# Two adjacency pairs kept on chip over the turn of a two-pass graph kernel, and one pair moved from the fourth step to the first

## The chip, the cores and the metric

The kernel runs on one core of one Trainium2 chip. The metric is the device time of one execution in microseconds, the median over several runs; lower is better.

## What is computed

The graph has 4096 nodes of 64 features and a dense 4096 x 4096 f32 adjacency matrix (64 MB). The reference, cut to what matters:

```python
def _ggc(x, adj, W, wih, whh, bih, bhh):
    m = adj @ (x @ W)
    gi = m @ wih.T + bih ; gh = x @ whh.T + bhh      # each split in three: r, z, n
    r = sigmoid(i_r + h_r); z = sigmoid(i_z + h_z); n = tanh(i_n + r * h_n)
    return (1.0 - z) * n + z * x

# layer 0: two passes over adj, with a residual and a layernorm
h = relu(_ggc(x, adj, W1, ...)) ; x = layernorm(x + relu(_ggc(h, adj, W2, ...)))
# layer 1: decayed weights of the last 100 neighbours of each row
support = x @ weight ; mask = adj != 0 ; rank = cumsum(mask, axis=1)
k = minimum(rank[:, -1:], 100) ; pos = rank - (deg - k)
w = mask * where(pos > 0, 0.5 ** (k - pos), 0)
x = layernorm(x + w @ support + bias)
```

## The kernel before, in words

The adjacency doesn't fit on the chip, so it is streamed. It is cut in 8 chunks of 512 output nodes, each chunk in 16 **pairs**; a pair is 256 source nodes by 512 output nodes, 512 KB of f32, and it is what one DMA loads and what one product of TensorE takes (four matmul records and four weight loads, helper `pair`, L445 to L451). `LOADS` (L74) lists all loads in order and `LOAD_AT` gives the place n of a pair in it. Load n goes to slot n % 7 of `stream`, a ring of seven slots. SyncE issues all of them (`load`, L390): load n waits until the pair n - 7 has been multiplied (`pair_used`), and in pass 1 until its mask has been made as well. The loads are in one queue and SyncE issues them strictly in this order.

**Pass 1** (loads 0 to 127) goes through chunks 0 to 7. For each pair VectorE (or, for some, ScalarE by a Sign and a Square) makes the 8-bit mask `codes`, and TensorE multiplies the pair with the first state `s_in`. The second state `s_mid` of a chunk is ready one chunk later, so pairs with source nodes below `2 * TRI[b]` are at once multiplied with it too, which saves a second load (L457 to L466). In chunk 7, pairs 0 to 11 are used twice in this way; pairs 12 to 15 of chunk 7 are not.

**The turn** (`TURN`, L72, and L607 to L614) is the first part of pass 2: twelve pairs in an order written out by hand. The tuple (s, q) is step s of pass 2, that is chunk 7 - s, pair q. It begins with (0, 12) and (0, 13), two pairs of chunk 7, which are loaded again as loads 128 and 129. Between its products lie `gates(7)`, `count(7)` and `node(7)`, the end of pass 1's last chunk.

**Pass 2** goes backwards through the chunks, with the loads 140 to 203, in six steps `chunk2(t)` (L616 to L627). Step t first runs `gates(7 + t)`, then `ALONG_PAIRS[t]` products, with `node(7 + t)` after the fourth of them. From step 2 on, four shares of layer 1's product (`share`, L540; each 16 matmuls of 128x128 f16) go with them, two ahead of the first product and two ahead of the fifth. Before: `{1: 8, 2: 10, 3: 12, 4: 12, 5: 11, 6: 11}`. A product needs its load, and steps run over chunk borders freely; so the counts say only how many pairs lie between two gates. After step 6 come 44 more shares, with the last two gates and nodes among them (L631 to L636).

What joins the engines around one chunk g of pass 2:

- TensorE's `gates(g)` (L497, matmuls of L509 and L516) waits for `m_ready` (VectorE, `combine`, L979), `state_made` (ScalarE, L701), `h_made` (VectorE, L1010) and, for g of 9 and up, `x1_made` (VectorE, `make_x1s`, L1073).
- ScalarE then makes the sigmoids `rz` (L678), VectorE `t_n` (L988, L992), ScalarE tanh (L685), VectorE `new_h` (L999 to L1004) and `residual` (L1010), which writes `h_c`.
- TensorE's `node(g)` (L522, L531) needs `h_c`; ScalarE squares it (L721), VectorE sums it (L1062, L1066), GpSimd takes the power (L851), VectorE makes `x1s` (L1073), ScalarE and VectorE split it (L731, L1089).
- Between these VectorE works off a written-out list of `chain` steps (L955, L960: the running count over the rows, and the codes) and ScalarE and VectorE expand codes to weights for the shares (L741 and L1100). Each engine takes its list strictly in order; VectorE's per-step list is at L1121 to L1142, ScalarE's at L799 to L811.

`RES_AT` (L105) sets after which load SyncE issues the small load `x_res` that `residual` needs.

On-chip memory that the change touches: `wexp` holds two buffers for expanded weights; its first half serves as `sums` in pass 1, its second half is used from step 1 of pass 2 on. `h_c` (L236), `sq` (L237) and `x1s` (L238) are 1, 1 and 2 KB per partition, 4 KB in all, the size of a pair per partition, and are written from step 1 of pass 2 on.

Of the kernel before, what the change touches and what calls it, by code (L numbers as in the profile page):

```python
# [17 lines left out]
P = 128  # L18
# [52 lines left out]

TURN = [(0, 12), (0, 13), (1, 10), (1, 11), (1, 12), (1, 13), (2, 10), (0, 14), (0, 15),  # L72
        (1, 14), (1, 15), (2, 11)]
LOADS = [(b, q) for b in range(NCH) for q in PAIRS[b]] + [(NCH + s, q) for s, q in TURN] + \  # L74
        [(NCH + s, q) for s in range(2, NCH) for q in range(2 * TRI[NCH - 1 - s], NP)
     if (s, q) not in TURN]
LOAD_AT = {pair: n for n, pair in enumerate(LOADS)}
# [21 lines left out]

ALONG_PAIRS = {1: 8, 2: 10, 3: 12, 4: 12, 5: 11, 6: 11}
FIRST = [NCH * NP, *(NCH * NP + len(TURN) + sum(ALONG_PAIRS[u] for u in range(1, t))
                     for t in range(1, NCH))]
RES_AT = [FIRST[1], *(n + SLOTS + 3 for n in FIRST[1:NCH - 1]), len(LOADS)]  # L105

# [64 lines left out]
OUT_ACT = (0, 2, 4)  # L171


def signed(n):
    return n % NP in BY_SIGN.get(n // NP, ())

# [28 lines left out]
def build(nc, adj_t, x_pairs, w1, consts, bias, out):  # L205
    with ExitStack() as ctx:
# [3 lines left out]
        def sem(name):  # L210
            return ctx.enter_context(nc.semaphore(name))
# [21 lines left out]
        zh = r_g  # L233
        n_g = sb("n_g", [P, HW], F32)
        x_res = sb("x_res", [P, HW], F32)
        h_c = sb("h_c", [P, HW], F32)  # L236
        sq = sb("sq", [P, KT, D], F32)  # L237
        x1s = sb("x1s", [P, KT, 2, D], F32)  # L238
        x1, sup_f = x1s[:, :, 0, :], x1s[:, :, 1, :]
        stat = sb("stat", [P, NCH, KT], F32)  # L240
        var = sb("var", [P, NCH, KT], F32)
# [82 lines left out]
        def support(j):  # L324
# [6 lines left out]
                at = s_mid[:, 0:CW].bitcast(F16)[:, (j - 6) * CW:(j - 5) * CW]  # L331
            return at.rearrange("p (k h d) -> p k h d", h=2, d=D)

        def edges(c, b, first, n):

            at = (c * NCH + b) * BLK + first * CW
            return codes[:, at:at + n * CW]
# [21 lines left out]
        x_in = [sem(f"x_in{i}") for i in range(len(X_IN))]  # L359
        w1_in, consts_loaded, bias_in = sem("w1_in"), sem("consts_loaded"), sem("bias_in")  # L360
        adj_in = [sem(f"adj_in{i}") for i in range(SLOTS)]
        pair_used, mask_made, sum_made = sem("pair_used"), sem("mask_made"), sem("sum_made")
        signs_read, squares_made = sem("signs_read"), sem("squares_made")
        s_bf_made, count_done, start_made = sem("s_bf_made"), sem("count_done"), sem("start_made")
# [23 lines left out]
        @blk.sync  # L388
        def _(sp):
            def load(n):  # L390
                g, q = LOADS[n]
                if n >= SLOTS:
                    sp.wait_ge(pair_used, n - SLOTS + 1)
                    if n - SLOTS < NCH * NP:
                        by_dve, by_sign = masks_before(n - SLOTS + 1)
                        if signed(n - SLOTS):
                            sp.wait_ge(signs_read, by_sign)
                        else:
                            sp.wait_ge(mask_made, by_dve)
                sp.dma_start(stream[:, n % SLOTS, :], adj_t[g if g < NCH else 2 * NCH - 1 - g, q])\  # L400
                    .then_inc(adj_in[n % SLOTS], 16)

            def load_res(s):
                ch, g = NCH - 1 - s, NCH + s
                if s > 0:
                    sp.wait_ge(h_made, g)
                sp.dma_start(x_res[:, :], x_pairs[:, bass.ts(ch, HW)]).then_inc(x_c_in, 16)

            for b in range(NCH):
                for q in range(NP):  # L410
                    load(b * NP + q)
                    if b == BIAS_AT - 1 and q == NP - 1:
                        sp.dma_start(bias_b[:, :, :].rearrange("p k d -> p (k d)"), bias)\
                            .then_inc(bias_in, 16)
            for n in range(NCH * NP, len(LOADS)):
                load(n)
                for s in range(NCH):
                    if n == RES_AT[s]:
                        load_res(s)
            load_res(NCH - 1)  # L420
            for i in range(NCH):
                if i in OUT_ACT:
                    sp.wait_ge(o_by_act, OUT_ACT.index(i) + 1)
                else:
                    sp.wait_ge(o_by_dve, i + 1 - sum(a < i for a in OUT_ACT))
                sp.dma_start(out[NCH - 1 - i], o_n[:, i]).then_inc(out_stored, 16)
            sp.wait_ge(out_stored, 16 * NCH)

        @blk.tensor
        def _(pe):  # L430
# [12 lines left out]
                last.then_inc(xw_done, 1)  # L443

            def pair(n, q, state, to, start, stop):  # L445
                for u in range(2):
                    t = 2 * q + u
                    last = nc.tensor.matmul(to[D * u:D * (u + 1), :], state[:, t * D:(t + 1) * D],  # L448
                                            stream[:, n % SLOTS, u * CW:(u + 1) * CW],
                                            start=start[u], stop=stop)  # L450
                return last  # L451

            def product1(b, q):
                n = LOAD_AT[b, q]
                pe.wait_ge(adj_in[n % SLOTS], 16 * (n // SLOTS + 1))
                last = pair(n, q, s_in, m_acc[b % 2], [q == PAIRS[b][0]] * 2, q == PAIRS[b][-1])
                twice = [p for p in PAIRS[b] if p < 2 * TRI[b]]  # L457
                if q in twice:
                    first = q == twice[0]
                    pe.wait_ge(s_mid_made, q // 2 + 1)  # L460
                    if first:
                        if b == 5:
                            pe.wait_ge(to_sup_made, 4)
                        if b in M2_AFTER:
                            pe.wait_ge(m2_kept, KEPT.index(M2_AFTER[b]) + 1)
                    last = pair(n, q, s_mid, m2_bank(b), [first] * 2, q == twice[-1] and b in KEPT)  # L466
                last.then_inc(pair_used, 1)

            def product2(s, q):
                g, ch = NCH + s, NCH - 1 - s  # L470
                n = LOAD_AT[g, q]
                first = s >= 3 and q == 2 * TRI[ch]
                pe.wait_ge(s_mid_made, q // 2 + 1)
                if first:

                    pe.wait_ge(m_ready, {3: NCH, 4: NCH - 1}.get(s, s + 7))
                pe.wait_ge(adj_in[n % SLOTS], 16 * (n // SLOTS + 1))
                pair(n, q, s_mid, acc_bank(g), [first] * 2, n == USED[g] - 1).then_inc(pair_used, 1)
                if first and ch in KEPT:
                    half, _, at = kept_part(ch)  # L480
# [158 lines left out]
        def _(act):  # L639
# [16 lines left out]
            def sign_mask(b, q):  # L656
                n, p = b * NP + q, PAIRS[b][q]
                to = edges(p // 2, b, 2 * (p % 2), 2)
                act.wait_ge(adj_in[n % SLOTS], 16 * (n // SLOTS + 1))
                nc.scalar.activation(to.bitcast(I8), stream[:, n % SLOTS, :], ACT.Sign)\  # L660
                    .then_inc(signs_read, 1)
                act.wait_ge(signs_read, masks_before(n)[1] + 1)
                nc.scalar.activation(to, to.bitcast(I8), ACT.Square).then_inc(squares_made, 1)
# [195 lines left out]
        def _(dve):  # L859
# [47 lines left out]

            def mask(b, q):
                n, p = b * NP + q, PAIRS[b][q]
                dve.wait_ge(adj_in[n % SLOTS], 16 * (n // SLOTS + 1))  # L910
                nc.vector.tensor_scalar(edges(p // 2, b, 2 * (p % 2), 2), stream[:, n % SLOTS, :],  # L911
                                        0.0, None, ALU.not_equal).then_inc(mask_made, 1)

            def sum_quads(b, part):
# [305 lines left out]
```

## Time and profile before

| | us |
|---|---|
| median of 3 runs | 353.23 |
| lowest and highest run | 352.85, 354.26 |
| the profiled execution, its own time | 352.96 |
| its span, first to last instruction | 351.2 |
| granted TensorE clock over the span | 0.998 of 2.4 GHz |

The time of the profiled execution is 1.8 us over its span; these lie outside the program's instructions. How to read the rows: busy times and starts are in microseconds from the start of the span, mean durations in ns. PE is the matmul side of TensorE, PEld its weight loads, DVE VectorE, ACT ScalarE, POOL GpSimd, SP SyncE. L448 is line 448 of the kernel. In a timeline a row is a run of instructions of one kind; the brackets at its end give the idle time of the engine ahead of it and what ended it, and a row without brackets followed the one before it with no idle time to speak of. Matmuls are pipelined, their ends are modelled and a pair's records overlap the next pair's, so the spacing of starts tells the rate, not the duration.

### The profile page before, as it was taken

What the parts mean: (1) busy time and instruction counts of PE and PEld (TensorE: products, weight loads), DVE (VectorE), ACT (ScalarE), POOL (GpSimd) and SP (SyncE); (2) the same over time, 40 slices, a digit from 0 to 9 for tenths busy, and PEclk for the clock granted to TensorE, in tenths of its full rate; (3) what the DMA queues carried; (4) which work ended last, traced back from release to release, by engine and by line L of the source; (5) the groups of instructions that cost most, each with busy time, mean ns of one, the idle gap of its engine ahead of it and who ended that gap; (6) DMA issues with size and microseconds to landing.
All of it is one profiled execution on the core that took longest, in us unless ns stands there. A gap on an engine that the chain in (4) does not pass through costs nothing. (4 is left out here: it accounts for less than half of the span.)

```text
span 351.2 us, 6769 instructions
## 1 busy us (share of the span) xinstructions
PE 329.9 (94%) x2536; PEld 154.2 (44%) x2536; DVE 302.4 (86%) x510; ACT 180.7 (51%) x235; POOL 24.8 (7%) x32
## 2 busy tenths in 40 slices
PE   1997999999999999999999999999999999979992
PEld 0441323233333333333333324444444454869992
DVE  0689879898999999997995667899899999888996
ACT  0202403114031140367467448977996969676993
POOL 2000000000000000000000001202020202022044
PEclk9999999999999999999999999999999999999999
DMA  7999999999999999999899999999999995000012
GB/s 243 413 411 410 410 407 409 409 409 397 405 361 331 392 377 363 365 318 342 294 359 316 376 411 406 406 350 326 358 380 370 383 383 215 17 1 4 2 32 91
DMA packets 32720, 111.10 MB, mean 316 GB/s; under 512 B 3632, under 2 KB 6192, under 8 KB 32688
## 3 DMA queue, kind: packets, MB, share of 16 engines
q1 hardware_dynamic: 31824, 109.20, 82.2%
q10 hardware_dynamic: 864, 1.48, 1.2%
q8 instruction: 20, 0.33, 0.4%
q14 instruction: 12, 0.10, 0.1%
HBM read 109.62 MB, written 1.05 MB: 315 GB/s over the span
## 5 line engine op out<-in xcount | busy, mean ns | idle before, releaser
L448 PE MATMUL m_acc<-stream,s_in 128*64 128x512 f32 x512 | 126.7, 603 | 4.0 <-DMA stream<-in_adj_t 3.1
L911 DVE TENSOR_SCALAR codes<-stream 128x1024 uint8<-128x1024 f32 x117 | 77.1, 686 | 6.6 <-DMA stream<-in_adj_t 6.3
L448 PE MATMUL out<-stream,s_mid 128*64 128x512 f32 x272 | 68.5, 593 | 0.2 <-DMA stream<-in_adj_t 0.2
L448 PEld LDWEIGHTS m_acc<-stream,s_in 128*64 128x64 f32 x512 | 34.4, 138 | 70.9 <-issue 47.9
L448 PE MATMUL m_acc<-stream,s_mid 128*64 128x512 f32 x240 | 55.2, 599 | 0.1
L851 POOL TENSOR_TENSOR rstd<-var,mhalf 128x4 f32<-128x4 f32 x16 | 23.0, 1436 | 322.7 <-DVE var L1066 322.7
L960 DVE SCALAR_TENSOR_TENSOR codes<-codes,run 128x384 uint32<-128x384 uint32 (+2 forms) x56 | 43.0, 768 | 1.9
L955 DVE TENSOR_TENSOR run<-run,codes 128x768 uint16<-128x768 uint16 (+2 forms) x55 | 41.5, 755 | 1.8
L646 ACT ACTIVATE m_high<-m_acc 64x512 f32<-64x512 f32 x13 | 7.7, 596 | 58.0 <-PE m_acc L448 45.1
L448 PEld LDWEIGHTS out<-stream,s_mid 128*64 128x64 f32 x272 | 19.5, 137 | 38.1 <-issue 37.4
L678 ACT ACTIVATE rz<-gate_ps,b_rz 128x256 f32<-128x256 f32 x32 | 13.4, 469 | 43.7 <-PE gate_ps L516 43.6
L741 ACT ACTIVATE wexp<-codes,code_bias 128x2048 uint16<-128x2048 uint8 x15 | 29.8, 1996 | 0.1
L741 ACT ACTIVATE codes<-codes,code_bias 128x2048 uint16<-128x2048 uint8 x15 | 29.6, 1989 | 0.0
L448 PEld LDWEIGHTS m_acc<-stream,s_mid 128*64 128x64 f32 x240 | 15.8, 136 | 28.9 <-issue 27.7
L928 DVE TENSOR_TENSOR wexp<-wexp,codes 128x2048 uint16<-128x2048 uint16 x16 | 19.6, 1225 | 6.5 <-issue 6.0
L509 PE MATMUL gate_ps<-mx,const 128*64 128x256 f32 x128 | 16.8, 381 | 2.1 <-DVE x1s L1073 2.0
L509 PEld LDWEIGHTS gate_ps<-mx,const 128*64 128x64 f32 x128 | 9.5, 137 | 13.2 <-issue 9.3
L685 ACT ACTIVATE n_g<-t_n,const 128x256 f32<-128x256 f32 x16 | 8.2, 511 | 13.3 <-DVE t_n L992 12.9
L1100 DVE TENSOR_SCALAR codes<-codes 128x2048 uint16<-128x2048 uint8 x12 | 14.3, 1221 | 0.0
L701 ACT ACTIVATE mx<-hx 64x256 f32<-64x256 f32 x32 | 13.3, 416 | 0.8
L863 DVE COPY s_in<-gate_ps 128x256 f32<-128x256 f32 x8 | 3.4, 420 | 11.3 <-PE gate_ps L440 11.3
L988 DVE SCALAR_TENSOR_TENSOR t_n<-gate_ps,const,rz 128x256 f32<-128x256 f32 x16 | 7.7, 481 | 6.1 <-ACT rz L678 5.9
(139 smaller groups left out, 375.2 us busy)
## 6 DMA issues: line engine op xcount, KB each, us to landing
stream<-in_adj_t SPq DMA_DIRECT2D x204, 512.0 KB, 6.4
x_res<-in_x_pairs SPq DMA_DIRECT2D x8, 128.0 KB, 6.8
out_nodes<-stream SPq DMA_DIRECT2D x8, 128.0 KB, 2.1
hx<-in_x_pairs ACTq DMA_DIRECT2D x1, 512.0 KB, 7.5
const<-in_consts ACTq DMA_DIRECT2D x1, 358.0 KB, 6.7
hx<-in_x_pairs ACTq DMA_DIRECT2D x2, 128.0 KB, 6.1
hx<-in_x_pairs ACTq DMA_DIRECT2D x1, 256.0 KB, 8.8
bias_b<-in_bias SPq DMA_DIRECT2D x1, 128.0 KB, 5.4
```

What stands on the lines that cost most here:

```text
L448: last = nc.tensor.matmul(to[D * u:D * (u + 1), :], state[:, t * D:(t + 1) * D], stream[:, n % SLOTS, u * CW:(u + 1) * CW], start=start[u] ...
L509: nc.tensor.matmul(to[e * D:(e + 1) * D, 0:HW], w_rz[layer][:, part * D:(part + 1) * D], mx[:, e * HW:(e + 1) * HW], start=True, stop=True)
L678: nc.scalar.activation(rz[:, bass.ts(part, HW)], (r_ps, z_ps)[part], ACT.Sigmoid, bias=b_rz[:, 2 * layer + part:2 * layer + part + 1])\
L685: nc.scalar.activation(n_g[:, :], t_n[:, :], ACT.Tanh, bias=b_ni[:, layer:layer + 1]).then_inc(n_made, 1)
L701: nc.scalar.activation(mx[D:P, e * HW:(e + 1) * HW], state_of(g)[e * D:(e + 1) * D, :], ACT.Copy)\
L741: nc.scalar.activation(weights(j, i).bitcast(U16), block(j, i), ACT.Relu, bias=code_bias[:, :], scale=float(P)).then_inc(by_act, 1)
L851: nc.gpsimd.tensor_tensor(rstd[:, r, :], var[:, r, :], mhalf[:, :], ALU.pow) .then_inc(rstd_made, 1)
L911: nc.vector.tensor_scalar(edges(p // 2, b, 2 * (p % 2), 2), stream[:, n % SLOTS, :], 0.0, None, ALU.not_equal).then_inc(mask_made, 1)
L928: nc.vector.tensor_tensor(to, left, right, ALU.add).then_inc(sum_made, 1)
L955: nc.vector.tensor_tensor(running(n + 1, U16)[:, to], running(n, U16)[:, to], tile_edges(c, k, U16)[:, to], ALU.subtract)\
L960: nc.vector.scalar_tensor_tensor(at, at, EDGE_BIT, running(n, U32)[:, to], ALU.logical_shift_left, ALU.bitwise_or)\
L1100: nc.vector.tensor_scalar(weights(j, i).bitcast(U16), block(j, i), float(P), -float(P * CODE_ZERO), ALU.mult, ALU.add)\
```

## The change

Pairs 12 and 13 of chunk 7 are loaded in pass 1 not into the ring but each into a place of its own: pair 12 into the second half of `wexp`, pair 13 into a new tile `late` of 4 KB per partition, of which `h_c`, `sq` and `x1s` become parts. The two loads of pass 2 for them go, 202 loads are left. The held loads have semaphores of their own, SyncE issues them without waiting for a slot, and their products in the turn neither wait for a load nor count as used. `landing(n)` counts what has been loaded into a slot, since the held loads leave theirs out. Products, masks and their order in pass 1 and in the turn are the same. `ALONG_PAIRS` goes to nine pairs in step 1 and eleven in step 4; steps 2 and 3 keep their counts, so that each of their pairs is the next one in the order.

```diff
+HELD = (12, 13)
+HELD_AT = [(NCH - 1) * NP + PAIRS[NCH - 1].index(q) for q in HELD]
+TURN_LOADS = [(NCH + s, q) for s, q in TURN if (s, q) not in [(0, p) for p in HELD]]
-LOADS = [(b, q) for b in range(NCH) for q in PAIRS[b]] + [(NCH + s, q) for s, q in TURN] + \
+LOADS = [(b, q) for b in range(NCH) for q in PAIRS[b]] + TURN_LOADS + \
...
-ALONG_PAIRS = {1: 8, 2: 10, 3: 12, 4: 12, 5: 11, 6: 11}
-FIRST = [NCH * NP, *(NCH * NP + len(TURN) + sum(ALONG_PAIRS[u] for u in range(1, t))
+ALONG_PAIRS = {1: 9, 2: 10, 3: 12, 4: 11, 5: 11, 6: 11}
+FIRST = [NCH * NP, *(NCH * NP + len(TURN_LOADS) + sum(ALONG_PAIRS[u] for u in range(1, t))
...
+def landing(n):
+
+    return 16 * sum(m not in HELD_AT for m in range(n % SLOTS, n + 1, SLOTS))
...
-        h_c = sb("h_c", [P, HW], F32)
-        sq = sb("sq", [P, KT, D], F32)
-        x1s = sb("x1s", [P, KT, 2, D], F32)
+        late = sb("late", [P, PW], F32)
+        h_c = late[:, 0:HW]
+        sq = late[:, HW:2 * HW].rearrange("p (k d) -> p k d", d=D)
+        x1s = late[:, 2 * HW:4 * HW].rearrange("p (k h d) -> p k h d", h=2, d=D)
+        held = [wexp[:, 1, :].bitcast(F32), late[:, :]]
...
+        def loaded(n):
+
+            if n in HELD_AT:
+                return held[HELD_AT.index(n)]
+            return stream[:, n % SLOTS, :]
+
+        def pair_in(engine, n):
+            if n in HELD_AT:
+                engine.wait_ge(held_in[HELD_AT.index(n)], 16)
+            else:
+                engine.wait_ge(adj_in[n % SLOTS], landing(n))
...
+        held_in = [sem(f"held_in{i}") for i in range(len(HELD))]
...
             def load(n):
                 g, q = LOADS[n]
+                if n in HELD_AT:
+                    at = HELD_AT.index(n)
+                    sp.dma_start(held[at], adj_t[g, q]).then_inc(held_in[at], 16)
+                    return
                 if n >= SLOTS:
...
             def pair(n, q, state, to, start, stop):
+                data = loaded(n)
...
-                                            stream[:, n % SLOTS, u * CW:(u + 1) * CW],
+                                            data[:, u * CW:(u + 1) * CW],
...
             def product2(s, q):
                 g, ch = NCH + s, NCH - 1 - s
+                if s == 0 and q in HELD:
+                    pe.wait_ge(s_mid_made, q // 2 + 1)
+                    pair(LOAD_AT[ch, q], q, s_mid, acc_bank(g), [False] * 2, False)
+                    return
                 n = LOAD_AT[g, q]
...
-                pe.wait_ge(adj_in[n % SLOTS], 16 * (n // SLOTS + 1))
+                pair_in(pe, n)
```

The waits and operands of the products of pass 1 and of the masks (L455, L659, L910) go through `pair_in` and `loaded` in the same way.

## Rows read from the trace of the kernel before

**Rows 1.** The page: engines' busy time in us, share of the span, instructions.

```profile
PE 329.9 (94%) x2536; PEld 154.2 (44%) x2536; DVE 302.4 (86%) x510; ACT 180.7 (51%) x235; POOL 24.8 (7%) x32
```

**Rows 2.** Windows: length, busy (x records) of PE, PEld, DVE, ACT, POOL; clock; DMA share; GB/s.

```profile
192.00:216.00 24.00, 23.48 (x136) 7.52 (x132) 16.89 (x39) 12.44 (x20) 1.14 (x1) 1.00 1.01 393
...
206.00:216.20 10.20, 9.83 (x58) 2.94 (x55) 7.74 (x19) 7.20 (x10) 1.14 (x1) 1.00 1.03 410
```

**Rows 3.** Waits of PE from 190 to 300 us: total, times, longest (all there are).

```profile
PE gate_ps L509 <- DVE x1s L1073: 0.4, 1, 0.4
PE out L448 <- DMA stream<-in_adj_t: 0.2, 1, 0.2
```

**Rows 4.** Chain of waits: start, length, what; products between two gates.

```profile
242.96 5.30 PE m_acc L448 x24
...
260.46 6.16 PE m_acc L448 x28
```

**Rows 5.** Timeline of PE, end of the turn and step 1 of pass 2.

```profile
204.12 1.08 PE L448 MATMUL out<-stream,s_mid 128*64 128x512 f32 x4 [0.21 <-DMA stream<-in_adj_t]
205.31 1.08 PE L509 MATMUL gate_ps<-mx,const 128*64 128x256 f32 x8
...
210.62 0.72 PE L531 MATMUL gate_ps<-to_x1s,h_c 64*128 64x128 f32 x8
...
212.85 2.96 PE L448 MATMUL m_acc<-stream,s_mid 128*64 128x512 f32 x12
216.17 1.08 PE L509 MATMUL gate_ps<-mx,const 128*64 128x256 f32 x8 [0.37 <-DVE x1s L1073]
```

**Rows 6.** Timeline of DVE, the same stretch: `combine(8)` and `make_x1s(0)`.

```profile
204.59 0.67 DVE L979 TENSOR_TENSOR mx<-out,m_high 64x512 f32<-64x512 f32 x1
...
215.34 0.68 DVE L1073 TENSOR_TENSOR x1s<-gate_ps,rstd 128x512 f32<-128x512 f32 x1
```

**Rows 7.** Pair loads: 22 issued 190 to 220 us; one at 208.9; one at 179.6.

```profile
DMA to landing us min/median/max: 5.1/6.9/9.1
...
DMA to landing us min/median/max: 7.0/7.0/7.0
...
DMA to landing us min/median/max: 4.4/4.4/4.4
```

**Rows 8.** Timeline of DVE, steps 2 to 7: the rows with a wait, and `n_input(14)`.

```profile
218.77 0.48 DVE L988 SCALAR_TENSOR_TENSOR t_n<-gate_ps,const,rz 128x256 f32<-128x256 f32 x1 [1.04 <-ACT rz L678]
...
224.44 0.42 DVE L1062 TENSOR_REDUCE stat<-sq 128x4 f32<-128x256 f32 x1 [0.44 <-ACT sq L721]
...
252.16 0.48 DVE L988 SCALAR_TENSOR_TENSOR t_n<-gate_ps,const,rz 128x256 f32<-128x256 f32 x1 [0.64 <-ACT rz L678]
...
267.34 1.22 DVE L1100 TENSOR_SCALAR codes<-codes 128x2048 uint16<-128x2048 uint8 x1
268.66 0.48 DVE L988 SCALAR_TENSOR_TENSOR t_n<-gate_ps,const,rz 128x256 f32<-128x256 f32 x1
...
274.67 0.42 DVE L1062 TENSOR_REDUCE stat<-sq 128x4 f32<-128x256 f32 x1 [0.16 <-ACT sq L721]
...
301.55 0.48 DVE L988 SCALAR_TENSOR_TENSOR t_n<-gate_ps,const,rz 128x256 f32<-128x256 f32 x1
```

**Rows 9.** Timeline of ACT: `sigmoids(11)`, one expansion, `sigmoids(14)`.

```profile
251.67 0.81 ACT L678 ACTIVATE rz<-gate_ps,b_rz 128x256 f32<-128x256 f32 x2
...
288.24 2.01 ACT L741 ACTIVATE wexp<-codes,code_bias 128x2048 uint16<-128x2048 uint8 x1
...
299.41 0.84 ACT L678 ACTIVATE rz<-gate_ps,b_rz 128x256 f32<-128x256 f32 x2 [0.56 <-PE gate_ps L516]
```

**Rows 10.** Timeline of PE: end of `gates(11)`; after the last product, `gates(15)` and `node(15)`.

```profile
250.20 0.66 PE L516 MATMUL gate_ps<-mx,const 64*64 64x256 f32 x8
...
310.49 1.08 PE L509 MATMUL gate_ps<-mx,const 128*64 128x256 f32 x8 [1.64 <-DVE x1s L1073]
...
316.35 0.71 PE L531 MATMUL gate_ps<-to_x1s,h_c 64*128 64x128 f32 x8 [0.51 <-DVE h_c L1010]
```

More of the change, by code:

```diff
@@ L476, in product2 @@
                     pe.wait_ge(m_ready, {3: NCH, 4: NCH - 1}.get(s, s + 7))
-                pe.wait_ge(adj_in[n % SLOTS], 16 * (n // SLOTS + 1))
+                pair_in(pe, n)
                 pair(n, q, s_mid, acc_bank(g), [first] * 2, n == USED[g] - 1).then_inc(pair_used, 1)
@@ L658, in sign_mask @@
                 to = edges(p // 2, b, 2 * (p % 2), 2)
-                act.wait_ge(adj_in[n % SLOTS], 16 * (n // SLOTS + 1))
-                nc.scalar.activation(to.bitcast(I8), stream[:, n % SLOTS, :], ACT.Sign)\
+                pair_in(act, n)
+                nc.scalar.activation(to.bitcast(I8), loaded(n), ACT.Sign)\
                     .then_inc(signs_read, 1)
@@ L909, in mask @@
                 n, p = b * NP + q, PAIRS[b][q]
-                dve.wait_ge(adj_in[n % SLOTS], 16 * (n // SLOTS + 1))
-                nc.vector.tensor_scalar(edges(p // 2, b, 2 * (p % 2), 2), stream[:, n % SLOTS, :],
+                pair_in(dve, n)
+                nc.vector.tensor_scalar(edges(p // 2, b, 2 * (p % 2), 2), loaded(n),
                                         0.0, None, ALU.not_equal).then_inc(mask_made, 1)
```

## The prediction

> **What bounds the kernel now.** I began with the page: PE is busy for 94% of the span, DVE for 86% [rows 1], so one of these two sets the time nearly everywhere, and DMA matters only where it makes one of them wait. The windows come next: through the turn and step 1 (192 to 216 us) the DMA engines are fully busy at 393 to 410 GB/s [rows 2], so here the removed loads could count. Then I asked what PE waited for in pass 2. There is little: 0.2 us for a pair's load and 0.4 us for DVE's `x1s`, each once, in 110 us [rows 3]. Last I followed DVE: from 224.44 to 301.55 its row of work has two waits in it, 0.64 us at 252.16 and 0.16 us at 274.67 [rows 8]. So PE and DVE run beside each other, both nearly full, and a gain on one counts only as far as the other lets it through. That is the main point of what follows.
>
> **Who sets the end.** PE starts `node(15)` at 316.35 after waiting for DVE's `h_c`, and `gates(15)` at 310.49 after waiting 1.64 us for DVE's `x1s` [rows 10]. Both hang on the chain that starts with `n_input(14)` on DVE at 301.55. That one did not wait: it has no bracket, and its sigmoid had started at 299.41, 2.1 us before [rows 8, 9]. DVE itself was late there. So the last 50 us move with DVE's start of `n_input(14)`, not with the end of PE's last product.
>
> **Part 1, the held pairs in pass 1.** Masks and products are the same in number and shape, from another address; 0. The two held loads are issued earlier than before (no slot wait) in a stretch where a load lands 4.4 us after its issue (the third of [rows 7]) and PE never waits; 0. If a held load did delay a neighbour by its own length, 1.3 us, PE's lead there would have to be gone first.
>
> **Part 2, two loads less in the turn.** A pair is 524288 bytes; at 410 GB/s [rows 2] that is 1.28 us, so the queue carries 2 x 1.28 = 2.56 us less. What reaches the loads behind is less. Loads for the next seven pairs go into slots freed in pass 1, and come two places, 2.56 us, earlier. But the pair after those, (1, 14), goes into the slot that (1, 10) frees, and that product is where it was. Before, it also had that slot. It is issued at the same time as before, and so is all behind it. It can only lose its queueing: it landed 5.1 us after its issue (the smallest of the 22 in [rows 7]), and an unqueued load takes 4.4 us. So from there on loads land 0.7 us earlier, not 2.56. Between 0 (if the queue is no shorter) and 0.7 I take 0.7, by the nearer row, as the queue is empty for a moment there.
>
> What does that bring PE? The product at 204.12 waited 0.21 us for its load [rows 5]. That wait goes. But `gates(8)` at 205.31 stands right behind `combine(8)` on DVE, 204.59 + 0.67 = 205.26 [rows 5, 6], and that stands behind DVE's chain steps, which no load touches. So the 0.21 us are given back in front of `gates(8)`: 0. `node(8)` at 210.62 and `x1s` at 215.34 hang on `gates(8)` alone: unmoved.
>
> The Trainium skill speaks of a shorter load than the row: "SBUF — State Buffer", section The DMA setup-cost knee, gives a transfer as about 2 us plus its bytes at 436 GB/s, 3.2 us for this size. By that, an estimate, loads behind the turn would land 1.9 us earlier and not 0.7; the trace has 4.4 us for one that waits for nothing, so it does not agree. The sum would be the same by either, only the slower rival below would lose most of its chance.
>
> **Part 3, the ninth pair in step 1.** A product costs PE (6.16 - 5.30) = 0.86 us [rows 4]. After `node(8)` the last three products start at 212.85 and 0.86 us apart; PE is through at 212.85 + 3 x 0.86 = 215.43, with small overheads 215.6, and waits until 216.17 for `gates(9)`, where DVE's `x1s` ends at 215.34 + 0.68 = 216.02 [rows 5, 6]. So PE has a hole of 0.55 to 0.6 us (the row shows 0.37, as a matmul record ends later than the next could start). A product of 0.86 us put into it ends at 212.85 + 4 x 0.86 = 216.29, with the overhead of about 0.05 216.34. `gates(9)` thus starts 0.17 us later: +0.17. Its load is the one issued at 208.9, landing at 215.9 before (the second of [rows 7]), at 215.2 after; it is needed at 215.5. It fits by 0.3 us.
>
> DVE's `n_input(9)` at 218.77 had waited 1.04 us for the sigmoids [rows 8], so it takes over the 0.17, and so does the sum of squares at 224.44 (it waited 0.44 for `node(9)`). From there DVE runs without a wait to 251.5: it is +0.17 all along. The wait at 252.16 gives nothing back: the sigmoid before it, at 251.67, has no bracket, so ScalarE came straight from an expansion [rows 9], and that row of expansions began with DVE's `x1s`. Steps 2 and 3 in all: +0.17.
>
> **Part 4, one pair less in step 4.** PE's `gates(12)` comes 0.86 us earlier, less the 0.17: -0.7. What does DVE take of that? At 268.66 `n_input(12)` follows an expansion from 267.34 of 1.22 us, which overlaps with the next by 0.08 elsewhere, so it could have started at 268.47: 0.19 us. At 274.67 it waited for the square behind `node(12)`, 0.16 us by the row, 0.25 with the same overlap [rows 8]. Behind that there is no wait on DVE up to 301.55 [rows 8]. So DVE can take at most 0.19 + 0.25 = 0.44 us of PE's 0.7, and keeps it to the end. The rest becomes idle time of PE: shares of step 6 use an expansion that ends only at 288.24 + 2.01 = 290.25 [rows 9], and ScalarE starts it by DVE's pace, and after 300 us PE waits for `h_c` and `x1s` longer.
>
> Moved with the pairs: `x_res` loads follow the same pairs or one later, and two or more steps of DVE lie before their use; 0. One pair is multiplied earlier in steps 1 to 3, so its successor's load has a slot 0.86 us earlier as well. Should a load in step 3 stall PE all the same, by up to 0.8 us it would only shrink PE's -0.7 and not reach DVE: `gates(11)` ends at 250.20 + 0.66 = 250.86 [rows 10], and ScalarE comes to its sigmoid at 251.67 [rows 9]. ScalarE's `high` and DVE's `combine` find their chunks done one pair earlier or at the same time, and the power on GpSimd waits for DVE alone: 0.
>
> **Sum.** DVE: +0.17 - 0.44 = -0.27 us, against 352.96 us of the profiled execution: 352.7. The median of the runs before is 0.27 us above that execution, so the median expected is 353.23 - 0.27, about 352.9. What a measurement of this kernel can tell from no change is about 0.5%, 1.8 us, so this is no change.
>
> **The rivals.**
>
> *PE sets the end after all* (0.15). If DVE's list is looser than its rows look (its durations overlap by up to 0.08 us, in some 60 instructions), then PE's 0.7 us comes through: 352.5. For it: PE is unbroken from 216 to 300 us. Against it: the 2.1 us by which the sigmoid of step 7 lay ready.
>
> *DMA sets the pace* (0.05). The loads run through pass 2 at the rate of full engines; if they did bound it, the whole 2.56 us would come off: 350.7. "Perfetto Trace Analysis" of the Trainium skill, section Roofline, puts the ceiling of one core at about 435 GB/s, and by that rule the 393 to 410 GB/s of the turn are near the bound. Against it stands the 0.2 us that PE waited for loads in pass 2 [rows 3]; the trace disagrees with this rule's outcome.
>
> *The ninth pair comes too late, and the kernel gets slower* (0.2). Place: the last product of step 1. If the loads are not earlier at all (the queue as before), its load lands at 215.9, PE takes it some 0.1 us later, and `gates(9)` starts at 216.9: +0.7 us, and everything up to the end hangs on `gates(9)` through DVE. With the 0.44 taken back in step 4 that is +0.3, 353.5. Loads of this stretch took up to 9.1 us [rows 7], 2.1 more than this one; with half of that on it the sum is +1.3, 354.5. It decides from a landing after 215.5 on, 0.3 us later than I expect it. For it: a margin of 0.3 us only. Against it: the queue must be shorter by two loads somewhere.
>
> **How the numbers follow.** The forecast (-0.27) has 0.6; its own range is 352.5 to 353.3. Rivals 0.15, 0.05 and 0.2. The range reaches from 352.1 (rival 1 with the spread of the medians, 0.4 us) to 353.9 (rival 3 with its smaller price and the same spread). Faster by over 0.5%: 0.05 from DMA and 0.02 for what I have not seen; slower by over 0.5% only in rival 3 beyond its larger price: 0.03. The rest, 0.90, is within 0.5%.
>
> **What would show it.** Right: no PE wait for a load in the turn; `gates(8)` at the same time; `gates(9)` 0.1 to 0.3 us later, with no wait before it; the last product 0.4 to 0.7 us earlier, but `n_input(14)` only 0.2 to 0.3 us earlier; more PE idle time before `node(14)` and `gates(15)`. Wrong: a wait for a load at the ninth pair; `gates(8)` earlier; `n_input(14)` earlier by 0.6 or more; any DVE wait in steps 5 to 7.

## The result and the profile after

The changed kernel takes 354.73 us (median of 8 runs, 354.56 to 355.27) against 353.34 us before (8 runs): a ratio of 1.0038, with a 95% interval of 1.0025 to 1.0051. It is 1.4 us slower, inside the half per cent that counts as no change, but outside the predicted range, and with the other sign. The profiled execution has 354.69 us of its own, its span is 353.0 (before 352.96 and 351.2). The ratios here and below leave out three executions that lie far off the rest (495 us in e1, 879 us in e9, 1931 us of the kernel before beside e13 and e14).

The page of the changed kernel, engines' busy time, shows that the work is the same as in [rows 1]:

```profile
PE 329.6 (93%) x2536; PEld 154.2 (44%) x2536; DVE 302.4 (86%) x510; ACT 180.5 (51%) x235; POOL 24.8 (7%) x32
```

What it waits for is not. PE's waits from 190 to 300 us in the changed kernel, to be held against [rows 3]:

```profile
PE m_acc L476 <- DMA stream<-in_adj_t: 1.7, 2, 0.9
PE gate_ps L541 <- DVE mx L1011: 0.6, 1, 0.6
PE out L595 <- ACT wexp L773: 0.2, 1, 0.2
PE m_acc L476 <- issue: 0.2, 1, 0.2
```

Two loads less, and PE now waits 1.7 us for loads where it had waited 0.2. The larger of the two waits, 0.92 us, is that of the ninth pair of step 1; the other, 0.76 us at the end of step 3, did no harm, since DVE's `n_input(11)` behind it waits 0.63 us as before (0.64). (Line numbers have moved: 476 is the product, 541 and 548 the gates, 516 the kept sums' product, 563 the node, 1020 `n_input`, 1094 the sum of squares.) The timeline of PE at the end of the turn and in steps 1 and 2 answers to [rows 5]:

```profile
205.05 1.08 PE L541 MATMUL gate_ps<-mx,const 128*64 128x256 f32 x8 [0.55 <-DVE mx L1011]
...
212.57 2.96 PE L476 MATMUL m_acc<-stream,s_mid 128*64 128x512 f32 x12
216.44 1.08 PE L476 MATMUL m_acc<-stream,s_mid 128*64 128x512 f32 x4 [0.92 <-DMA stream<-in_adj_t]
217.32 1.06 PE L541 MATMUL gate_ps<-mx,const 128*64 128x256 f32 x8
...
220.80 3.65 PE L476 MATMUL m_acc<-stream,s_mid 128*64 128x512 f32 x16
224.38 0.65 PE L516 MATMUL m_acc<-kept,ident 64*64 64x256 f32 x4
224.96 0.72 PE L563 MATMUL gate_ps<-to_x1s,late 64*128 64x128 f32 x8
```

Everything up to `gates(8)` is 0.26 us earlier than before, `gates(7)` too (193.33 against 193.59). Executions differ by that much before they reach the turn, so I count from `gates(7)` below. Two things are to be seen. The ninth product of step 1 starts at 216.44, 0.92 us after PE had nothing else to do. And in step 2 the product of the kept sums (L516) stands ahead of `node(9)` (L563): four products, then L516, then the node. Before, it stood behind it (L484 is the product, L531 the node):

```profile
223.26 0.72 PE L531 MATMUL gate_ps<-to_x1s,h_c 64*128 64x128 f32 x8
...
225.79 1.08 PE L448 MATMUL m_acc<-stream,s_mid 128*64 128x512 f32 x4
226.80 0.65 PE L484 MATMUL m_acc<-kept,ident 64*64 64x256 f32 x4
```

The timeline of DVE, the rows with a wait and two `n_input` rows, to be held against [rows 8]:

```profile
219.55 0.48 DVE L1020 SCALAR_TENSOR_TENSOR t_n<-gate_ps,const,rz 128x256 f32<-128x256 f32 x1 [2.09 <-ACT rz L710]
226.14 0.42 DVE L1094 TENSOR_REDUCE stat<-late 128x4 f32<-128x256 f32 x1 [1.36 <-ACT late L753]
...
253.78 0.48 DVE L1020 SCALAR_TENSOR_TENSOR t_n<-gate_ps,const,rz 128x256 f32<-128x256 f32 x1 [0.63 <-ACT rz L710]
260.10 0.42 DVE L1094 TENSOR_REDUCE stat<-late 128x4 f32<-128x256 f32 x1 [0.48 <-ACT late L753]
...
270.67 0.48 DVE L1020 SCALAR_TENSOR_TENSOR t_n<-gate_ps,const,rz 128x256 f32<-128x256 f32 x1
...
303.28 0.48 DVE L1020 SCALAR_TENSOR_TENSOR t_n<-gate_ps,const,rz 128x256 f32<-128x256 f32 x1
```

The sum of squares of step 2 waits 1.36 us for its node (before 0.44), and there is a wait of 0.48 us at the same place of step 4 (260.10) that did not exist. `n_input(14)` is at 303.28 and not at 301.55, +1.73; the span is 1.7 longer. The end still hangs on it: in all profiles of this study but one it lies 49.68 to 49.70 us behind `n_input(14)`, and 49.73 in that one.

**Where the saved transfers went.** Windows of the kernel before and of the changed kernel over the turn; the columns are those of [rows 2]. Before:

```profile
195.00:197.00 2.00, 2.00 (x15) 0.75 (x12) 0.90 (x2) 1.34 (x3) 0.00 (x0) 1.00 0.99 401
197.00:201.00 4.00, 4.00 (x26) 1.49 (x24) 2.60 (x7) 2.72 (x6) 0.00 (x0) 1.00 1.00 404
201.00:206.00 5.00, 4.67 (x24) 1.37 (x22) 3.81 (x9) 0.60 (x1) 0.00 (x0) 1.00 1.02 408
```

After:

```profile
195.00:197.00 2.00, 2.00 (x12) 0.76 (x14) 1.09 (x3) 1.33 (x4) 0.00 (x0) 1.00 0.47 188
197.00:201.00 4.00, 4.00 (x28) 1.48 (x26) 2.66 (x7) 2.46 (x6) 0.00 (x0) 1.00 0.94 303
201.00:206.00 5.00, 4.45 (x26) 1.31 (x22) 3.57 (x8) 0.59 (x1) 0.00 (x0) 1.00 0.99 362
```

The difference is 2 x 213 + 4 x 101 + 5 x 46 = 1060 KB, two pairs. The transfers that were taken away became an idle queue at 195 us, and then a queue that restarts slowly; by 206 us the kernel has moved two pairs less than before, just those that were taken away, and the loads land when they did.

### The profile page after: what moved, and what is told of

The parts are those of the page before. It is cut to its first block and busy times, and to the rows that moved or that the text cites. A ratio compares the mean times of both kernels' runs of the same rounds, so it can differ in the third digit from the quotient of the medians.

```text
span 353.0 us, 6763 instructions
## 1 busy us (share of the span) xinstructions
PE 329.6 (93%) x2536; PEld 154.2 (44%) x2536; DVE 302.4 (86%) x510; ACT 180.5 (51%) x235; POOL 24.8 (7%) x32
## 5 line engine op out<-in xcount | busy, mean ns | idle before, releaser
L476 PE MATMUL m_acc<-stream,s_in 128*64 128x512 f32 x504 | 124.8, 604 | 3.9 <-DMA stream<-in_adj_t 3.1
L476 PE MATMUL out<-stream,s_mid 128*64 128x512 f32 x264 | 66.5, 593 | 0.0
```

## The experiments

For each run the table gives, for its profiled execution: its own time; the landing of the ninth pair of step 1, chunk 4's pair 12, and the start of `gates(9)`, both counted from `gates(7)`; from there to step 2's sum of squares; and from that to `n_input(12)`. Then the ratio to the kernel before over all runs, with its interval.

| | own | landing | gates(9) | to squares | to n_input(12) | ratio |
|---|---|---|---|---|---|---|
| before | 352.96 | 22.29 | 22.58 | 8.26 | 44.22 | |
| change | 354.69 | 22.98 | 24.00 | 8.82 | 44.52 | 1.0038 (1.0025 to 1.0051) |
| e1 hold only | 352.78 | 22.74 | 22.59 | 8.26 | 44.04 | 0.9992 (0.9978 to 1.0006) |
| e2 move only | 353.95 | 22.32 | 23.33 | 8.82 | 44.53 | 1.0064 (1.0040 to 1.0087) |
| e3 kept sums behind node | 354.91 | 23.34 | 24.35 | 9.11 | 43.96 | 1.0015 (1.0001 to 1.0030) |
| e4 held pairs later | 354.79 | 22.73 | 23.74 | 8.82 | 44.53 | 1.0028 (1.0013 to 1.0043) |
| e5 more waits | 355.64 | 23.11 | 24.12 | 8.82 | 44.52 | 1.0062 (1.0038 to 1.0085) |
| e6 change, node after 3 | 353.31 | 22.56 | 23.57 | 7.68 | 44.60 | 1.0020 (1.0002 to 1.0037) |
| e7 before, node after 3 | 353.19 | 22.50 | 22.58 | 8.04 | 44.77 | 1.0012 (0.9997 to 1.0028) |
| e8 e4 and e6 | 352.90 | 21.66 | 22.67 | 7.94 | 44.34 | 0.9996 (0.9985 to 1.0007) |
| e9 e8, pair from step 2 | 352.44 | 21.06 | 22.62 | 7.99 | 43.96 | 0.9983 (0.9966 to 1.0000) |
| e10 change, again | 355.86 | 24.24 | 25.25 | 8.82 | 44.52 | one run |
| e11 move only, again | 354.59 | 22.60 | 23.62 | 8.88 | 44.52 | one run |
| e12 as e5, other semaphore | 355.35 | 23.04 | 24.05 | 8.82 | 44.52 | 1.0068 (1.0048 to 1.0089) |
| e13 ninth without load | 353.69 | 22.84 | 22.63 | 8.79 | 44.53 | 1.0028 (1.0016 to 1.0041) |
| e14 e13, kept sums behind | 353.59 | 23.41 | 24.01 | 8.24 | 43.95 | 1.0007 (0.9996 to 1.0017) |

The columns nearly tell it by themselves: where the ninth pair is in step 1, and loaded, `gates(9)` comes 1.01 or 1.02 us after its landing in all but one (in e9 the load is in time); 8.8 stands where the kept sums' product is ahead of `node(9)`, about 8.25 where it is behind and nothing else waits.

**e1: hold, move nothing.** The counts are those of before.

```diff
-ALONG_PAIRS = {1: 9, 2: 10, 3: 12, 4: 11, 5: 11, 6: 11}
+ALONG_PAIRS = {1: 8, 2: 10, 3: 12, 4: 12, 5: 11, 6: 11}
```

> The two pairs are held, the counts of the steps stay 8, 10, 12, 12. Theory A (the loss sits in the moved pair: its load comes late, and the product with the kept sums, 0.58 us, slips ahead of node(9)): no change against before, within 0.3 us; gates(8), gates(9) and n_input(14) where they were, relative to gates(7), and the product at the end of the turn without its wait of 0.2 us. Theory B (holding itself costs, by the addresses or by the queue that runs empty at 196 us): slower than before by about the 1.4 us of the change.

0.9992, no change: theory B falls. Holding costs nothing and brings nothing. Its product at the end of the turn still waited 0.2 us for a load, so theory A was not right in that either.

**e2: move, hold nothing.** The reverse edit in the kernel before.

> Nothing is held, the kernel before with nine pairs in step 1 and eleven in step 4. Theory A: as slow as the change, 1.0 to 2.0 us over before; the ninth pair waits for its load, 0.5 to 1.3 us, and node(9) comes 1.1 to 1.8 us later. Theory C (holding did bring the loads 0.7 us forward, and the rest of the loss is elsewhere): 0.7 us slower than the change, 2.1 us over before.

1.0064: the moved pair alone is the loss. The size, 2.3 us by the medians (355.28 against 352.98), was theory C's and above A's; C's reason isn't borne out, since the ninth pair's load landed no later here (22.32) than with holding (22.98). Its profiled execution was the fastest of its six; the second look, e11, came out nearer the others. Whether holding makes the moved pair cheaper (1.0038 against 1.0064, with intervals that overlap) these runs don't settle: the landing is 22.3 and 22.6 us without holding, 22.98 and 24.24 with it.

**e3: the kept sums' product behind the node.** The four matmuls that add the kept sums are no longer issued with the chunk's first product but ahead of the next one, so behind a node that falls between:

```diff
                 if first and ch in KEPT:
-                    half, _, at = kept_part(ch)
-                    pe.wait_ge(m2_kept, len(KEPT))
...
+                    kept_due.append((g, ch))
...
                     if n == NODE_AT[t]:
                         node(NCH + t - 1)
+                    add_kept()
```

> The change, with the product of the kept sums put behind node(9), node(10) and node(11) in place of ahead of them. Theory A: node(9) and the sum of squares behind it come 0.55 us earlier than in the change, and since VectorE waited there, so does the end: 0.5 us faster than the change. Theory D (only the late load counts): as slow as the change within 0.2 us.

1.0015 against 1.0038, 0.8 us by the ratios, with intervals that overlap a little: it speaks against theory D, the product counts. This profile is that of its slowest run, with another late load of 0.65 us ahead of `node(9)`, so its 9.11 hides the gain; the next column shows it, 43.96 against 44.52. The same product slips ahead of `node(11)` in step 4 as well. e14 shows both.

**e4: held pairs later in the turn.**

```diff
-TURN = [(0, 12), (0, 13), (1, 10), (1, 11), (1, 12), (1, 13), (2, 10), (0, 14), (0, 15),
+TURN = [(1, 10), (1, 11), (1, 12), (0, 12), (0, 13), (1, 13), (2, 10), (0, 14), (0, 15),
```

> The change, with the turn's two held pairs multiplied fourth and fifth in place of first and second, so that (1, 10), (1, 11) and (1, 12) free their slots about 3 us earlier. Theory A (the queue ran empty at 196 us because the held products free no slot, so the 2.56 us saved were lost as an idle queue): the queue stays full, loads of step 1 land 2 to 2.6 us earlier than in the change, the ninth pair does not wait, gates(9) is 1.2 us earlier, and the end 1.0 to 1.3 us earlier than in the change. Theory E (loads of that stretch are late for another reason, such as the engines being full): landings and time as in the change.

A part of it came. The load of (1, 15) landed 6.0 us after `gates(7)` and not 8.1, and that of (2, 11) at 7.3 and not 9.95, so the queue did stay full up to there, and theory E falls for this stretch. But (2, 12) was issued at 5.47 us as in the change and landed 3.5 us behind (2, 11): the queue had only run thin a place later. The lead was 0.85 us at (2, 12) and 0.56 at the eighth pair of step 1, since each load still has to wait for the product seven loads before it, and those products wait for gates and nodes, not for data. The ninth pair landed only 0.25 us earlier, 22.73, and the ratio is 1.0028, 0.35 us better and not 1.0 to 1.3.

**e5 and e12: where the instruction refill falls.** The profile of the changed kernel has one packet on the instruction queue in 213.9 to 214.5 us (columns: packets, MB, share of the 16 engines' time):

```profile
q1 hardware_dynamic: 66, 0.23, 96.0%
q8 instruction: 1, 0.02, 11.3%
```

There are 20 of these in the whole execution, 16 KB each and 0.9 to 1.1 us long on one DMA engine. The ninth pair's load was under way then, and it landed 2.0 us after its predecessor, where 1.28 is the rule. Two more waits per pair of pass 1 were to shift them:

```diff
+                    if b >= 1:
+                        pe.wait_ge(w1_in, 16)
+                        pe.wait_ge(w1_in, 16)
                     product1(b, PAIRS[b][q])
```

> The change, with two more waits ahead of each pair's products in chunks 1 to 7 of pass 1, on a semaphore that is long set. They hold nothing up; they only shift by some 224 instructions where TensorE's instruction stream is refilled (a 16 KB transfer on the instruction queue, at 214.1 us in the trace of the change). Theory F (such a refill, 1.1 us on one DMA engine, made the ninth pair's load late): the refill comes at about 217 us, that load lands 1.0 us after its predecessor's 1.3 us and not 2.0, the product waits under 0.4 us, and the time is 0.5 to 1.0 us below the change. Theory E (late for another reason): wait and time of the ninth pair as in the change, 0.9 us by the row and 354.7.

A miss. The refill came at 205.0 us, and the time got worse, 1.0062. There were 21 refills and not 20, which ties this queue to TensorE's instructions, the only ones that the edit adds. But the program as built has 2116 instructions for TensorE against 2004 of the change: one more for each pair and not two, as the other wait is carried by an instruction that was there already. A second kernel had the second wait on another semaphore, which was to give two each:

> The change with two waits on two different semaphores ahead of each pair of chunks 1 to 7 (in e5 the two were on one semaphore and became one, 112 instructions in all). Theory F: with 224 instructions the refills fall 32 instructions, some 3 us, later than in the change, at about 217.5 us and behind the ninth pair's load, whose product waits at most 0.3 us; time 353.6 to 354.2. Rival: where the refill falls isn't set by the instruction count, and it comes in front of the load as in the change: 354.7 or more.

Another miss, and the run isn't what was expected of it: this program too has 2116 instructions for TensorE, 112 more than the change and not 224. It repeats e5. The refill fell 13.7 us after `gates(7)`, at 207.6, ahead of the load once more; 1.0068. So a program with 224 more was never run, and I couldn't place a refill where I wanted it.

What the profiles say together is more. Counted from the landing of (2, 13), seven loads ahead, the ninth pair's load lands 8.9 to 9.0 us later in twelve of the sixteen profiles, that is at the pace of seven times 1.28. In the other four it takes 9.7 (change), 9.9 (e13), 10.05 (e4) and 10.5 us (e10), and these are the four in which a refill falls 19.4 to 20.8 us after `gates(7)`, while this load or the one ahead of it was under way. In the others the refill falls elsewhere and the gap with it: in twelve profiles, these four among them, a pair lands 1.9 to 3.2 us behind its predecessor, 2.2 to 3.3 us after a refill began. In the other four the refill of e14 has no such gap behind it, that of e3 begins when its gap is nearly over, and those of e5 and e12 fall ahead of (2, 13), which there lands 2.5 us behind (2, 12). So a refill goes with 0.7 to 1.5 us on the ninth pair's landing; it is not shown to be the cause, as no run moved it at will.

The rest of the spread lies in (2, 13) itself, which lands at 13.3 to 13.7 us without holding and at 12.2 to 14.5 with it. In e1, e3, e10 and e14 it came 2.7 to 3.0 us behind (2, 12), before 1.64, with no refill near. That is why e3 and e14 landed late (23.3 and 23.4) with no refill in the stretch.

**e10: the change again.**

> The changed kernel itself, a second execution under the profiler. If the refill of TensorE's instructions falls before the ninth pair's load again (214.1 us in the first profile, 219.7 in e6 with the same program up to there), that load is late again, 0.9 us of wait, and the time is about 354.7; if it falls after it, the wait is 0.2 us and the time 353.6 to 354.0.

A refill in the stretch again (19.9 us after `gates(7)`), and the load later still. PE of that profile waits twice:

```profile
216.33 1.08 PE L476 MATMUL m_acc<-stream,s_mid 128*64 128x512 f32 x4 [1.49 <-DMA stream<-in_adj_t]
217.62 1.08 PE L476 MATMUL m_acc<-stream,s_mid 128*64 128x512 f32 x4 [0.20 <-DMA stream<-in_adj_t]
```

**e11: move only, again.**

> e2's kernel again (nothing held, pair moved), since its profiled execution was its fastest (353.95 against a median of 355.28). Expected now: the ninth pair's load lands 1 us or more later than the 22.3 us after gates(7) of that profile, by a refill or a queue that was late before it, and the product waits 1 us or more.

Landing 22.60, 0.3 us later than in e2's profile and not 1 us; `gates(9)` 23.62, time 354.59. A miss in size, but with e2 it shows the floor: even a load that no refill makes late holds `gates(9)` up by 0.75 us (e2) to 1.04 us (e11) against 22.58.

**e6: node one product earlier, in the change.**

```diff
-NODE_AT = {1: 4, 2: 4, 3: 4, 4: 4, 5: 4, 6: 4}
+NODE_AT = {1: 4, 2: 3, 3: 3, 4: 3, 5: 4, 6: 4}
```

> The change, with node(9), node(10) and node(11) after three products of their step in place of four, so ahead of the chunk's first product and of the kept sums' product. Theory A: node(9) comes 0.86 + 0.58 us earlier, VectorE's sum of squares takes the 1.36 us it had waited for it, and the end is 1.0 to 1.4 us earlier than in the change, close to before. Theory D (only the late load counts): as slow as the change within 0.3 us.

The squares come 7.68 us behind `gates(9)` and not 8.82, as said, and the time falls to 1.0020, 0.65 us by the ratios where I had 1.0 to 1.4: A was too large. Over its own runs of the kernel before, the median is 1.08 us slower, where the change had 1.39; by that measure the gain is 0.3 us, on the edge of what D allows. The rows, not the time of this run, speak against D.

**e7: the same in the kernel before.**

> The kernel before with the same three nodes one product earlier. Theory A (VectorE sets the end from step 2 on, its wait of 0.44 us at the sum of squares of step 2 is the only one left): 0.4 to 0.5 us faster than before. Rival (TensorE sets the end): no change.

No gain: 1.0012, the outcome of the rival. The squares are earlier (8.04), but then DVE's `n_input(10)` waits where it had not waited:

```profile
233.99 0.48 DVE L988 SCALAR_TENSOR_TENSOR t_n<-gate_ps,const,rz 128x256 f32<-128x256 f32 x1 [0.35 <-ACT rz L678]
```

Its sigmoid follows `gates(10)` on PE. In step 2 both engines are at the end of their slack, and what is taken from one the other asks for: the 0.2 us that DVE gained at the squares is gone at `n_input(10)`, so DVE doesn't set the pace alone.

**e8: both.**

> The change with the held pairs fourth and fifth in the turn and the three nodes one product earlier. Theory A: both gains of e4 and e6 in one, 353.0 to 353.6, no slower than before. Rival: the gains overlap, since both shorten the same wait of VectorE: as e6.

0.9996: the loss of the change is gone, by 1.5 us. Here the ninth pair is on time, and the node stands ahead of the kept sums' product (L516):

```profile
213.06 3.73 PE L476 MATMUL m_acc<-stream,s_mid 128*64 128x512 f32 x16
216.59 1.06 PE L541 MATMUL gate_ps<-mx,const 128*64 128x256 f32 x8
...
220.07 2.79 PE L476 MATMUL m_acc<-stream,s_mid 128*64 128x512 f32 x12
222.80 0.71 PE L563 MATMUL gate_ps<-to_x1s,late 64*128 64x128 f32 x8
223.44 1.08 PE L476 MATMUL m_acc<-stream,s_mid 128*64 128x512 f32 x4
224.45 0.65 PE L516 MATMUL m_acc<-kept,ident 64*64 64x256 f32 x4
```

Four products in a row from 213.06, `gates(9)` 22.67 us after `gates(7)`: this is what the prediction had drawn for the change.

**e9: the pair taken from step 2.** As e8 with counts 9, 9, 12, 12, 11, 11.

> As e8 (held pairs fourth and fifth, three nodes one product earlier), but the ninth pair of step 1 is taken from step 2 and not from step 4: counts 9, 9, 12, 12. In e8 VectorE waited 0.28 us for the sigmoids of gates(10), so TensorE bound step 2; with a product of 0.86 us less there, that wait goes. Theory A: n_input(10) 0.25 to 0.3 us earlier than in e8 relative to gates(7), kept to the end, so 0.3 us under e8: 352.5. Rival: ScalarE's row of expansions or a late load takes it, no change against e8.

0.9983 (0.9966 to 1.0000), median 352.44 against 352.89: 1.9 us faster than the change by the ratios, and the only kernel of the study that may beat the one before, by a margin that its interval just reaches. DVE waits 0.2 us in all from 221 to 250.

**e13 and e14: the two terms taken out.** In e13 the ninth product reads 1024 columns of the second state, which is on chip, so it leaves out this pair's share of the result, and the wait for its load moves to the tenth, which then counts for both:

```diff
+                if (s, q) == (3, 12):
+                    pe.wait_ge(s_mid_made, NCH)
+                    pair(n, q, s_mid, acc_bank(g), [False] * 2, False, s_mid[:, 0:PW])
+                    return
+                if (s, q) == (3, 13):
+                    pair_in(pe, n - 1)
...
-                pair(n, q, s_mid, acc_bank(g), [first] * 2, n == USED[g] - 1).then_inc(pair_used, 1)
+                pair(n, q, s_mid, acc_bank(g), [first] * 2, n == USED[g] - 1)\
+                    .then_inc(pair_used, 2 if (s, q) == (3, 13) else 1)
```

> The change, but the ninth product of step 1 reads the second state in place of its pair, so that it needs no load (this product's values are not the adjacency's); its load is still made and is waited for one product later, behind gates(9). Theory A+F: gates(9) starts 22.7 us after gates(7), as the sum of the prediction had it (22.58 + 0.1 to 0.17), the sum of squares of step 2 8.8 us behind it; 0.9 to 1.3 us faster than the change, 353.1 to 353.7. Theory B' (the late load was in the profiles but isn't what the median is made of): within 0.3 us of the change.

`gates(9)` stands at 22.63, where the prediction's sum had it, with the pair's own load landing at 22.84. The time is 1.0028. That is 0.35 us below the change by the ratios, and 0.56 by the medians, each over its own runs of the kernel before (0.83 and 1.39); less than the 0.9 to 1.3 expected, more than B' allowed by the one measure and on its edge by the other.

> e13 with the kept sums' products put behind node(9) to node(11), as in e3. Theory A: the sum of squares of step 2 comes 8.25 us behind gates(9), as before the change, not 8.8; another 0.4 to 0.6 us faster than e13, so within 0.3 us of before: then the two terms together are the whole loss. If 0.3 us or more are left over before, a third term is missing.

1.0007, no different from before, and 0.75 us under e13, with intervals that just overlap. PE of e14 in step 2, with the node (L577) ahead of the kept sums' product (L530):

```profile
220.84 3.65 PE L476 MATMUL m_acc<-stream,s_mid 128*64 128x512 f32 x16
224.43 0.71 PE L577 MATMUL gate_ps<-to_x1s,late 64*128 64x128 f32 x8
225.07 0.65 PE L530 MATMUL m_acc<-kept,ident 64*64 64x256 f32 x4
```

DVE of e13 and then of e14, the sums of squares with a wait: in e13 the one of step 4 waits as in the change, in e14 there is no such row.

```profile
225.13 0.42 DVE L1101 TENSOR_REDUCE stat<-late 128x4 f32<-128x256 f32 x1 [1.03 <-ACT late L760]
...
259.09 0.42 DVE L1101 TENSOR_REDUCE stat<-late 128x4 f32<-128x256 f32 x1 [0.48 <-ACT late L760]
```

```profile
225.61 0.42 DVE L1109 TENSOR_REDUCE stat<-late 128x4 f32<-128x256 f32 x1 [0.78 <-ACT late L768]
```

(e14's own `gates(9)` came at 24.01 in this execution, though its ninth product needs no load: the loads of (2, 13) to (2, 15) were late, PE waited 0.2 us for each, and `node(8)` stood 18.15 us after `gates(7)` where e13 has 16.91. So the ninth pair isn't the only one of step 1 that a late stretch of the queue can hold up.)

The sum closes within its intervals: with the load and the kept sums' product taken out, nothing is left of the loss that can be told from zero. That the two together are the loss is clear of the noise (e14 and e8 against the change, whose intervals don't overlap); how it is shared between them is less so.

## Why the prediction was wrong

**What bounds the kernel: right for delays, not for gains.** DVE carries every delay from step 2 on. In every profile the end lies 49.7 us behind `n_input(14)`, and a late `gates(9)` reaches it in full. But time given back to DVE in step 2 doesn't reach the end, as TensorE's `gates(10)` is next (e7).

**Part 1, holding: right.** e1, 0.9992. The wait of 0.2 us ahead of `gates(8)` was worth nothing, as `combine(8)` set that time; the change's `gates(8)` waits 0.55 us for it.

**Part 2, "from there on loads land 0.7 us earlier": wrong.** It took the queue's two ends (5.1 us of latency, 4.4 for one that waits for nothing) and carried the difference through eleven loads. The lead was larger at first and then gone: counted from `gates(7)`, (1, 14) landed 2.0 us earlier than before, (1, 15) 1.0, (2, 11) 0.4, and from (2, 12) on none did. The load of (1, 14), issued at 196.00 in the changed kernel, took

```profile
DMA to landing us min/median/max: 3.2/3.2/3.2
```

But a queue that has run thin does not go on at 1.28 us per pair. The next ones landed 2.3, 1.8 and 1.7 us apart, at 303 to 362 GB/s. At the ninth pair the lead was less than nothing: it landed 0.7 us later than before. The 3.2 us is the estimate for this size by the fit in "SBUF — State Buffer" of the Trainium skill, The DMA setup-cost knee; the prediction had set it aside because the trace showed 4.4. By this row, the trace agrees with it. The 4.4 us row was misread: when that load was issued, at 179.6, three loads ahead of it had not landed, so it did wait for others.

**Part 3, "it fits by 0.3 us": wrong, and with Part 4 this is what turned the sign.** It rested on Part 2. The load issued at 208.63 in the changed kernel took 7.7 us, not 6.3:

```profile
DMA to landing us min/median/max: 7.7/7.7/7.7
```

so `gates(9)` was 1.42 us later, not 0.17. My third rival was this mechanism, at 0.2; it deserved most of the chance. Its first price, +0.7 for a load that is not earlier at all, is what e2 shows (0.75); the other 0.7 of the change came with the refill ahead of this load. Its own figures said so: without the lead, the load of before lands at 215.9 and is needed at 215.5. The filled hole of 0.55 us can be had only with a pair that is on chip, or loaded 1 us earlier (e8).

**Part 4, "-0.44", and "steps 2 and 3 in all: +0.17": wrong, by an operation that I did not count.** I moved a product, and took steps 2 and 3 as unchanged since their counts are. Their pairs are not the same ones: each step now begins one pair later in the order, so the first product of chunks 3, 2 and 1, which brings the product with the kept sums (0.58 us on PE), moved from the fifth place to the fourth, ahead of `node(9)`, `node(10)` and `node(11)`. DVE waited for `node(9)` and takes the 0.56 in full (8.82 against 8.26), and again in step 4, so that up to `n_input(12)` it is +0.30 and not -0.19. Of what I hoped for behind that, the 0.25 us at `sumsq(12)` did come. This step alone also makes the forecast's sign wrong: e13, with the late load taken out, is still 1.0028.

**The sum again**, for the profiled pair, counted from `gates(7)`: +1.42 at `gates(9)`, +0.56 at `node(9)`, +0.30 to `n_input(12)`, -0.28 from there to `n_input(14)`: +2.00; 0.26 less for the earlier `gates(7)`, +1.74 against 1.73 measured. Over many executions e13 and e14 give about 0.35 to 0.55 us to the late load and 0.75 to the kept sums' product; so a typical execution probably paid less for the late load than the 1.42 us of the profiled one.

**Not settled:** whether the refill of TensorE's instructions makes a load late or only goes with it; why (2, 13) lands up to 1.1 us later than before in some executions with holding, with no refill near; why e5 and e12, whose refills fall far ahead of the ninth pair, are slower than the change (1.0062 and 1.0068 against 1.0038).

## What to carry to other kernels

When a schedule is shifted by one item, write out each step's new list and look at what is glued to its items: here a product of 0.58 us changed sides with a node that another engine waited for. A transfer that is removed helps a later one only if something lets that one start earlier; in a ring whose slots are freed by products at fixed times, it turns into an idle queue. And a hole in an engine's row is only as useful as the data that can be there in time: work out the landing of the very item first, from the worst of its neighbours.

## What the runs showed of the hardware

- A load of 512 KB issued into a nearly empty queue (the one load ahead landed 0.65 us later) took 3.2 us, and 3.0 to 3.4 in the nine profiles that have this place; in pass 1, with three loads ahead that had not landed, one took 4.4, and the 22 of the turn and step 1 had 5.1 to 9.1, with a median of 6.9. After the queue had run thin at 195 us in the change, pairs landed 2.3, 1.8 and 1.7 us apart, before 1.28 was reached again.
- TensorE's instruction stream is refilled by 16 KB packets on a queue of its own, 0.9 to 1.5 us each on one of the 16 DMA engines; 112 instructions more made 21 of them out of 20 (e5, e12). In executions of one and the same program up to that point they fell at 19.9, 20.8 and 26.3 us after `gates(7)` (e10, the change, e6).
- A wait on a semaphore that has long been set doesn't always cost an instruction: of the 224 added in e5 and in e12, on one semaphore or on two, 112 became instructions of their own.
